# First values weighed ahead of the output projection, and two GpSimd operations held until VectorE's short routing steps are over

## What is computed

```python
mod = (_silu(c) @ wmod).reshape(8, 6, 1, -1)         # shifts, scales and gates of each batch
sa, ca, ga, sb, cb, gb = (mod[:, n] for n in range(6))
h = _layernorm(x) * (1 + ca) + sa
# attention: 16 heads of 8, key allowed where |q - k| <= 32
Q, K, V = split(einsum('bsd,ed->bse', h, W_qkv))
attn = softmax(where(mask, einsum('bhqd,bhkd->bhqk', Q, K) / sqrt(8), -inf))
x = x + ga * einsum('bsd,ed->bse', einsum('bhqk,bhkd->bhqd', attn, V), W_o)
h = _layernorm(x) * (1 + cb) + sb
# mixture of 8 experts of width 64: 4 groups of 2, best 2 groups, best 2 experts of them
scores = sigmoid(h @ gate_weight.T); choice = scores + bias
w = normalised scores of the 2 chosen experts, 0 for the others
y = sum over e of w[:, e] * (silu(h @ gate_proj[e].T) * (h @ up_proj[e].T)) @ down_proj[e].T
x = x + gb * y
```

## Time and profile before

| what | us |
|---|---|
| median of 3 runs | 168.95 (168.29 to 169.29) |
| the profiled execution | 168.28 |
| its span, first to last instruction | 166.5 |
| PE busy / PEld busy | 147.6 / 124.2 |
| DVE busy | 129.4 |
| ACT busy | 88.6 |
| POOL busy | 54.9 |

### The profile page before, as it was taken

The page is one execution under the profiler, slowest core; times in us unless marked ns, Lnnn a source line. Parts: engine busy times, 40 slices in busy tenths (PEclk is TensorE's granted clock), DMA queues, the critical chain, the costliest instruction groups (busy, mean ns, idle before and its releaser), DMA issues.

```text
span 166.5 us, 5054 instructions
## 1 busy us (share of the span) xinstructions
PE 147.6 (89%) x1966; PEld 124.2 (75%) x1968; DVE 129.4 (78%) x353; ACT 88.6 (53%) x173; POOL 54.9 (33%) x109
## 2 busy tenths in 40 slices
PE   6799986979899989999899989998999899966943
PEld 2478875868689968997699869985998599644833
DVE  3456457698989998889899989997989888763572
ACT  3143765356838473855477456845672555535220
POOL 6422130140063605370526143523412252163030
PEclk9999999999999999999999999999999999998799
DMA  5864241102330242013401330044003400100002
GB/s 143 234 191 28 24 41 12 34 1 35 22 47 0 32 32 69 6 31 20 78 4 16 35 48 4 4 46 52 0 4 41 57 0 4 33 0 0 0 0 63
DMA packets 47430, 6.21 MB, mean 37 GB/s; under 512 B 42416, under 2 KB 47024, under 8 KB 47408
## 3 DMA queue, kind: packets, MB, share of 16 engines
q1 hardware_dynamic: 47264, 5.90, 22.6%
q10 hardware_dynamic: 144, 0.00, 0.0%
HBM read 3.81 MB, written 2.10 MB: 35 GB/s over the span
## 4 chain that ended last, share of the span: by engine, by line
PE 58%; DVE 23%; issue 9%; ACT 7%; POOL 2%; POOLq 0%; ACTq 0%; DVEq 0%
PE ps L637 8%; PE ps L669 8%; PE ps L729 7%; DVE blkmax L936 5%; PE ps L597 3%; PE ps L652 3%; PE ps L722 3%; PE ps L787 3%; PE ps L756 3%; PE ps L707 3%; DVE shift L954 2%; PE ps L709 2%; PE ps L708 2%; PE ps L611 2%; PE ps L615 2%
## 5 line engine op out<-in xcount | busy, mean ns | idle before, releaser
L352 POOL TENSOR_TENSOR act_w<-act,cw 128x512 f32<-128x512 f32 x15 | 15.7, 1044 | 49.1 <-issue 33.5
L936 DVE TRANSPOSE_TENSOR_REDUCE blkmax<-ps 128x44 f32<-128x1408 f32 x16 | 26.3, 1642 | 4.9 <-PE ps L644 4.9
L486 ACT ACTIVATE probs<-ps 128x704 f32<-128x704 f32 x32 | 23.2, 754 | 6.8 <-PE ps L652 6.0
L669 PE MATMUL ps<-probs,v_bd 128*36 128x64 f32 (+2 forms) x640 | 23.3, 227 | 0.5 <-ACT probs L486 0.5
L669 PEld LDWEIGHTS ps<-probs,v_bd 128*36 128x36 f32 x640 | 20.9, 114 | 3.0 <-issue 0.9
L637 PEld LDWEIGHTS ps<-q_sb,k_bd 32*128 32x128 f32 x640 | 19.4, 186 | 4.7 <-issue 3.4
L637 PE MATMUL ps<-q_sb,k_bd 32*128 32x96 f32 (+2 forms) x640 | 21.3, 274 | 0.6 <-ACT probs L486 0.3
L493 ACT ACTIVATE o_t<-ps 36x512 f32<-36x512 f32 x16 | 9.5, 593 | 15.8 <-PE ps L669 15.7
L499 ACT ACTIVATE tanh_g<-ps 128x512 f32<-128x512 f32 x16 | 9.6, 597 | 15.4 <-PE ps L709 15.4
L729 PE MATMUL ps<-wd_sb,act_t 128*128 128x128 f32 x128 | 16.7, 276 | 0.7 <-ACT act_t L503 0.7
L729 PEld LDWEIGHTS ps<-wd_sb,act_t 128*128 128x128 f32 x128 | 15.9, 191 | 1.0 <-ACT act_t L503 0.9
(11 more groups left out here) (102 smaller groups left out, 281.5 us busy)
## 6 DMA issues: line engine op xcount, KB each, us to landing
x_sb<-x SPq DMA_DIRECT2D x8, 128.0 KB, 2.5
v_spill<-v_sb SPq DMA_DIRECT2D x8, 128.0 KB, 2.3
v_bd<-v_spill SPq DMA_DIRECT2D x32, 32.0 KB, 2.8
out<-out_sb SPq DMA_DIRECT2D x7, 128.0 KB, 2.4
wgu_sb<-w_gu SPq DMA_DIRECT2D x1, 512.0 KB, 4.3
wm_sb<-wmod SPq DMA_DIRECT2D x1, 256.0 KB, 3.8
wd_sb<-w_down SPq DMA_DIRECT2D x1, 256.0 KB, 5.4
con<-consts SPq DMA_DIRECT2D x1, 244.0 KB, 2.9
```

The costliest lines, as they stand in the source:

```text
L352: nc.gpsimd.tensor_tensor(act_w[:, t, :].rearrange("p (e i) -> p e i", e=E), act[:, t, :].rearrange("p (e i) -> p e i", e=E), view(cw[:, t ...
L486: nc.scalar.activation(probs[:, t, hgs, cols], ps[:, hgs, cols], ACT.Exp, scale=float(DH) ** -0.5).then_inc(probs_ready, 1)
L669: last = nc.tensor.matmul(ps[p0:p0 + VW, OB, c0 + lo * KB:c0 + (hi + 1) * KB], v_bd[:, i % VB, kb, hg, :], view(probs[:, t, hg, at:at + 1] ...
L936: nc.vector.tensor_reduce(blkmax[:, t, :, live(t):live(t) + LIVE], view(ps[:, 0, live(t) * KB:live(t) * KB + 1], [[BANK, NHG], [KB, LIVE], ...
```

## The change

Two things change, in the middle six steps. On TensorE `weigh_values(i, 0, 0)` moves from behind `scores(i, 1)` to the place between `transpose_on(i-1)` and `output_projection(i-1)`. On GpSimd `low_part(i)` of batches 1 to 6 gets a wait for the eighth routing step of the same batch, and `add_output(b)` of batches 0 to 5 a wait for `cw_ready` of batch b+1. No instruction is added, removed or resized.

```diff
@@ low_part and add_output, GpSimd
                 wait(pool, h2_hi_ready, i, 1, 1)
                 wait(pool, up_ps, i, NT, 0)
+                if 0 < i < B - 1:
+                    wait(pool, route_step, i, ROUTE, COMPARE_STEPS)
                 nc.gpsimd.tensor_tensor(h2_lo[:], h2_t[:], h2_hi[:].bitcast(F32), ALU.subtract)\
                   .then_inc(h2_lo_ready, 1)
 
             def add_output(b):
                 wait(pool, yg_ready, b, 1, 1)
+                if b < B - 2:
+                    wait(pool, cw_ready, b + 1, 1, 1)
                 wait(pool, out_stored, b, 16, 0)
@@ step, TensorE
                 transpose_on(i - 1)
+                weigh_values(i, 0, 0)
                 output_projection(i - 1)
                 up(i - 2, 1)
                 scores(i, 1)
-                weigh_values(i, 0, 0)
                 weigh_values(i, 0, 1)
```

## The result

The changed kernel takes 185.35 us, median of 4 executions (183.74 to 186.41), against 169.01 (168.29 to 169.29) before: 1.096 times as long, 95% interval 1.091 to 1.101, so 16.3 us or 9.6% slower. The prediction had 178.8 us with a range of 174.6 to 184.7. The direction was right, and so was the stall for the values; the fall of TensorE's clock, which the sum left out, was not, and the measured time lies 0.65 us above the range.

What follows compares the result with a forecast made beforehand. PE and DVE handing work to each other were taken to bound the six-step loop; 6.62 us lateness plus 4.08 us of calls minus 0.9 given back made 9.8, on 168.95 giving 178.8 us, range 174.6 to 184.7.

Steps and rivals of the forecast that it cites:

- The moved call meets its values too early: PE stands for the value DMAs before the moved call, delaying the output projection: 6.62 us lateness plus 4.08 us calls.
- Each step is charged anew: The value DMAs start from delayed work, so each of six steps pays its own lateness, 6.62 us together.
- What is given back: PE, with the call already done, reaches the transposes of `xn` sooner: 0.15 us per step, 0.9 for six.
- rival 2: Stalls in the loop lower PE's clock, falls in two steps adding 3.4 us: 182.2 us; chance 0.14.
- The two held operations: DVE's `wsel` and `allowed` save 0.34 and 0.18 us, worth nothing beside the stall; the GpSimd holds' costs stay hidden.
- Rival 1: Values reach PE's moved call in time, so each step gains 0.11 us: 168.3 us; chance 0.06.

Runs made afterwards that it cites:

- values_at_hand: Changed kernel, but the moved call reads the previous batch's already landed values and the wait for new values goes to the next weighing call; 170.92 us, ratio 1.0082.
- two_dmas: Changed kernel with only two of the four value DMAs for batches 2 to 7, TensorE waiting for two; 171.28 us, ratio 1.0064.
- fill5: Changed kernel with five useless 512-column bf16 matmuls in front of the moved call; 180.55 us, ratio 1.071.
- move_only: Changed kernel without the two GpSimd holds, so only the TensorE move; 184.76 us.
- holds_only: Changed kernel with the weighing call back at its old place, so only the two GpSimd holds; 169.33 us, ratio 0.9997.
- part_at_hand: Changed kernel, only four of the call's ten products ahead of the output projection, six at the old place, reading the previous batch's values; 169.72 us, ratio 1.0025.

## Why the prediction was wrong, step by step

**The moved call meets its values too early: right.** All six stalls are there and the landing releases them. From the earlier trace rows I had a call start at the landing and L756 0.68 us behind it; measured is the landing plus about 0.1 (0.06 to 0.12 in the six steps) and, at the full clock, 0.74 (step 2). values_at_hand and two_dmas show that this lateness is what costs.

**Each step is charged anew: right.** From the copied V to the end of the DMA chain the changed kernel takes as long as before. In step 3 it is 66.38 - 58.70 = 7.7 us. Read in the same way, steps 2 to 7 have 8.6, 7.7, 8.0, 7.6, 7.3 and 7.2 us; the earlier trace rows with the 2.8 us of the earlier trace rows and the spills of the same trace give 8.5, 7.5, 8.0, 8.2, 7.1 and 7.1 before.

**What is given back: wrong, 0.9 us.** I compared the end of `xn` with the end of L669 and took 0.15 of the 0.23 us between them as a gain. The handover from `xn` to the transposes takes 0.14 to 0.15 us, not the 0.05 that I had read off another pair (in step 5 of the kernel before `xn` ends at 100.64 + 0.88 = 101.52 and the transposes start at 101.67, 0.15 later: there was no slack). So the way over `xn` was already the one that ended last. From L760 to L601 it is 4.77 us in step 2 of the changed kernel, without the call in between, and 4.78 before with it. Without this term the sum is 10.7 us, and with 0.1 us of handover for each of six stalls 11.3; fill5, where the clock is kept up, has 180.55 - 169.16 = 11.4.

**The clock: this is the step that failed.** The sum had nothing for it: I had it as rival 2 with a chance of 0.14, for two falls, with steps 2, 4 and 5 as the liable ones. That the range reached 184.7 is no credit to it, as the upper end came from the lateness. The profiled execution has three falls, in steps 3, 4 and 5. What one costs I had nearly right: from the earlier trace rows 1.7 us. Measured in step 3: the call takes 0.40 us more, and from L760 to the spill of the next V it is 79.35 - 67.58 = 11.77 us, for 73.09 - 62.48 = 10.61 in step 3 of the kernel before, 1.16 more, so 1.6. That spill, before:

```profile
73.09 0.36 SPq L279 DMA_DIRECT2D v_spill<-v_sb  x1
```

For steps 4 and 5 the same sum gives 1.4 and 1.5. The three make 4.4 us, and the profiled executions of the changed kernel and of fill5 are 183.74 - 179.51 = 4.2 apart. The two longer falls of move_only cost more, 5.28 - 3.05 = 2.2 and 4.72 - 2.42 = 2.3 us (what steps 2 and 5 take more than before, less what the output projection comes later at the full clock). What I mis-sized was the chance. I had argued that busy work before and after a stall protects the clock, since in the earlier trace rows a slack stretch of several us stood ahead of the fall. It doesn't: in step 3 PE was busy for all of 62 to 64 and 0.69 of the next us, and the fall came behind one stall of 1.6 us:

```profile
62.00:63.00 1.00, 1.00 (x6) 0.71 (x5) 0.93 (x4) 0.83 (x2) 0.00 (x0) 1.00 0.56 33
63.00:64.00 1.00, 1.00 (x9) 0.94 (x8) 0.64 (x3) 0.66 (x2) 0.00 (x0) 1.00 0.39 24
64.00:65.00 1.00, 0.69 (x4) 0.20 (x2) 0.98 (x2) 0.78 (x2) 0.00 (x0) 1.00 0.71 41
```

The forecast should have carried some falls in it; put together afterwards, 169.0 + 11.3 + three at 1.5 us = 184.8.

The Trainium skill, "TensorE: Matmul & The Clock Gate", Part 1, says that activity releases the throttle and that how many matmuls a kernel starts with at the lower level differs from run to run. The stall of 2.77 us that kept the clock and the one of 2.78 that lost it are a variation of that kind, here in the middle of a kernel.

**The two held operations: right that they do nothing here, wrong why they would do nothing elsewhere.** I gave `wsel` a value of 0.17 us for each step in a world without the stall. holds_only shows 0.0: the 0.34 us reappear as VectorE's wait for L746. I had read "PE waits 0.17 us for DVE" in the earlier trace rows as VectorE being late, and it is the fixed length of a dependent pair.

**Rival 1: its sign was wrong.** I had 168.3 us for values in time. Measured is 1.4 us slower than before. Of my terms, 0.21 us for the later output projection was right (0.20), 0.15 given back and 0.17 from VectorE were both nothing, so a step loses 0.15 to 0.2 us (17.30 for 17.15) instead of gaining 0.11. In short: neither wait of PE that the change set out to fill was worth filling, as part_at_hand shows for the larger one.

What stays open is what decides which of the stalls takes the clock down. The profiled executions of the changed kernel and of move_only have twelve stalls: the five of 0.92 to 1.20 us all kept the clock, and of the seven of 1.54 to 2.78 us six lost it and one, of 2.77 us, kept it. Length has to do with it and doesn't decide it alone; no run here tells the stalls apart otherwise.

## What to carry to other kernels

When an instruction moves up in a queue, list every semaphore that it waits for and follow each back to its issue. A DMA that had slack where the instruction stood is a stall for all that is queued behind it, and in a loop where the DMA starts from that very work the stall is paid in every turn. A gap of an engine is worth filling only if the engine's own queue sets the length of the step; if a chain through other engines does, work moved into the gap leaves a wait of about the same length further on. If a change makes TensorE stand idle for 1.5 us or more at a time, as in the seven longer stalls here, count the falls of the clock as part of the forecast, not as a tail of it.

## What the runs showed that I had not expected

- A single stall of 1.5 to 1.9 us between stretches of full work brought TensorE's clock to 1.2 GHz for some 3 us of work, which cost about as much again as the stall: 1.4 to 1.6 us. Stalls of 2.15 and 2.78 us brought it down for nearly 7 us, at 2.2 to 2.3 us each, and one of 2.77 us in another execution not at all.
- Because of that the spread between executions grows: 180.44 to 187.27 us for move_only, where the kernel before has 168.2 to 171.0. Useless matmuls in the stall made the changed kernel 4.8 us faster.
- VectorE's product of a PSUM and an SBUF operand (`k_bd`) and GpSimd's subtraction (`h_lo`) ran side by side without either getting longer, 1.23 and 0.73 us, while `wsel` with two small SBUF operands was held by GpSimd's `out_sb` for 0.34 us.
